# A graph, attention and expert layer on one core: TensorE's loop over chunk pairs in the first phase is written out

## The reference

```python
xn = _layernorm(x)
# graph part: two GCN layers with A = counts of edges plus self loops, D = degrees
h = relu(D^-1/2 A D^-1/2 (xn @ W1.T) + b1)
g = D^-1/2 A D^-1/2 (h @ W2.T) + b2
# attention with 256 random features per head, 12 heads of 64
q, k, v = split(xn @ W_qkv)
phi(t) = exp(t @ rf.T - 0.5 * |t|^2) / 16
out = phi(q) @ (phi(k).T @ v) / (phi(q) @ sum(phi(k)) + 1e-6)
m = layernorm(xn + out @ W_proj + b_proj) * gamma + beta
x = x + g + m
# expert part: top-2 routing of 8 experts, the higher index wins
x = x + silu(layernorm(x) @ w1[e]) @ w2[e]
```

## Time and profile before

| | |
|---|---|
| median of 3 runs | 2528.85 us |
| lowest, highest | 2526.37, 2531.22 us |
| the profiled execution's own time | 2527.59 us |
| its span in the trace | 2525.8 us |
| mean granted TensorE clock | 0.975 |
| TensorE busy | 2350.2 us (93%) |
| VectorE busy | 1261.0 us (50%) |
| ScalarE busy | 870.3 us (34%) |
| GpSimd busy | 866.3 us (34%) |

### The profile page before, as it was taken

One profiled execution on the slowest core, in us unless ns is written; L12 is line 12 of the kernel. 1 busy time (PEld: TensorE's weight loads), 2 busy tenths in 40 slices (PEclk: granted clock), 3 DMA queues, 4 the chain that ended last, 5 costly groups with the idle time before them and its releaser, 6 DMA issues.

```text
span 2525.8 us, 45448 instructions
## 1 busy us (share of the span) xinstructions
PE 2350.2 (93%) x16783; PEld 1590.9 (63%) x16783; DVE 1261.0 (50%) x2843; ACT 870.3 (34%) x1323; POOL 866.3 (34%) x615
## 2 busy tenths in 40 slices
PE   5999899998999999998999999999996899999576
PEld 3878687877666666664665666666663566666365
DVE  6757475734667676674114334443331344444344
ACT  3646364634637465471122222222210011111142
POOL 1001116567777787775601111111100000000265
PEclk9999999999999999998999999999998999999799
DMA  7779685654232323325307776677745844454187
GB/s 290 270 265 309 208 272 151 181 134 99 16 63 1 63 7 56 51 13 138 43 10 238 224 218 209 212 219 226 215 180 199 251 163 154 165 174 172 57 167 128
DMA packets 172999, 392.22 MB, mean 155 GB/s; under 512 B 74864, under 2 KB 81882, under 8 KB 166460
## 3 DMA queue, kind: packets, MB, share of 16 engines
q1 hardware_dynamic: 90796, 320.38, 36.8%
q0 software_dynamic: 71264, 40.45, 14.5%
q10 hardware_dynamic: 10800, 29.50, 3.0%
HBM read 226.03 MB, written 169.71 MB: 157 GB/s over the span
## 4 chain that ended last, share of the span: by engine, by line
PE 77%; DVE 8%; ACT 8%; issue 4%; DMA 3%; SPq 0%; POOL 0%; DVEq 0%; ACTq 0%; POOLq 0%
PE pair L1842 31%; PE pair L374 30%; PE pair L1674 4%; PE pair L1654 2%; PE pair L1604 2%; DVE arena L1306 2%; DVE arena L1308 2%; DVE arena L1312 2%; ACT arena L912 2%; DMA arena<-ahl_dram 1%; PE pair L1986 1%; PE pair L1663 1%; PE pair L1973 1%; ACT arena L896 1%; PE pair L1773 1%
## 5 line engine op out<-in xcount | busy, mean ns | idle before, releaser
L374 PE MATMUL pair<-arena 128*128 128x384 f16 (+2 forms) x5760 | 906.2, 319 | 25.4 <-SPq L363 12.8
L718 POOL DMA_INDIRECT cells<-arena x392 | 654.6, 1670 | 574.3 <-DMA cells<-arena 437.6
L1842 PE MATMUL pair<-arena 128*128 128x384 f16 x4900 | 819.2, 328 | 34.5 <-DMA arena<-ahl_dram 19.8
L374 PEld LDWEIGHTS pair<-arena 128*128 128x128 f16 (+1 forms) x5760 | 567.1, 99 | 347.8 <-issue 24.4
L1842 PEld LDWEIGHTS pair<-arena 128*128 128x128 f16 x4900 | 475.3, 98 | 344.1 <-issue 21.2
L750 POOL DMA_INDIRECT slots<-arena x25 | 28.7, 1149 | 513.6 <-DVEq L1530 481.0
L1674 PE MATMUL pair<-arena 128*128 128x66 f32 x1200 | 157.9, 275 | 4.8 <-ACT arena L872 4.3
L1674 PEld LDWEIGHTS pair<-arena 128*128 128x128 f32 x1200 | 146.6, 192 | 13.8 <-ACT arena L872 12.0
L872 ACT ACTIVATE arena<-pair,arena 128x256 f32<-128x256 f32 x300 | 123.6, 472 | 64.6 <-PE pair L1654 62.1
L736 POOL DMA_DIRECT2D arena<-cells x25 | 30.3, 1213 | 336.4 <-DMA arena<-cells 329.7
L987 ACT ACTIVATE arena<-arena 128x768 f32<-128x768 f32 x25 | 23.4, 935 | 344.7 <-DVE arena L1409 344.7
(11 more groups left out here) (202 smaller groups left out, 2425.0 us busy)
## 6 DMA issues: line engine op xcount, KB each, us to landing
cells<-arena SPq DMA_DIRECT2D x50, 800.0 KB, 9.9
ahl_dram<-arena SPq DMA_DIRECT2D x25, 1600.0 KB, 10.9
arena<-ahl_dram SPq DMA_DIRECT2D x25, 1600.0 KB, 7.7
arena<-in_x SPq DMA_DIRECT2D x70, 384.0 KB, 3.7
arena<-key_dram SPq DMA_DIRECT2D x28, 896.0 KB, 5.8
arena<-cells SPq DMA_DIRECT2D x25, 800.0 KB, 7.6
arena<-cells POOLq DMA_DIRECT2D x25, 800.0 KB, 7.5
split_w<-arena SPq DMA_DIRECT2D x32, 384.0 KB
```

Of the source, the lines that this page charges most:

```text
L374: ins = nc.tensor.matmul(dst[half], left(k, a), right(k, b, half), start=start and n == 0, stop=stop and n == 2)
L718: nc.gpsimd.indirect_dma_start(cells[k], bass.IndirectOffsetOnAxis(ap=idx_all[:, m:m + 1], axis=0), val_all[:, m:m + 1], None, bounds_chec ...
L1842: ins = nc.tensor.matmul(pair[u][:, half, 0:HD], a[:, 0, s * P:(s + 1) * P], X[part][:, s, half * HD:(half + 1) * HD], start=(s == 0 and p ...
```

## The change

TensorE's first phase is written out for the five chunks, with the chunk's number as a constant. Nothing else in the source changes.

```diff
-            with pe.Fori(0, (C - 1) // 2) as i:
-                chunk1(2 * i, 0)
-                chunk1(2 * i + 1, 1)
-            chunk1(C - 1, 0, False)
+            for c in range(C):
+                chunk1(c, c % 2, c + 1 < C)
             finish_phase(pe, 0)
```

## The result

| | before | after |
|---|---|---|
| median | 2529.15 us (5 runs) | 2513.65 us (5 runs) |
| lowest, highest | 2526.37, 2531.22 | 2512.74, 2516.51 |
| profiled execution, own time | 2527.59 | 2516.24 |
| its span | 2525.8 | 2514.5 |
| ratio | | 0.9942, 95% interval 0.9928 to 0.9957 |

The change makes the kernel faster by 0.58%, that is 10.9 to 18.2 us by the interval.

The account below looks back on a forecast made before the run. TensorE was taken to bound the kernel; 7.00 + 1.83 + 0.8 = 9.63 us off the profiled 2527.59 gave 2517.96, and 1.26 for the median of the runs made 2519.2 us. The range was 2515 to 2524 us.

Parts of the forecast that it names:

- What bounds the kernel: Whole kernel: TensorE is the bound, 77% of the chain, so time it gains in phase 1 is gained at the end.
- The jump back: Phase 1, border of chunks 1 and 2: TensorE's idle time at the loop's one taken jump goes, 7.00 us.
- The slow start: Chunk 2's first block of 216 matmuls, at half clock behind the jump, takes 34.31 instead of 36.14 us: 1.83 us gained.
- The opening: Start of phase 1: the loop's opening branch no longer delays the first matmul after the last weight split, 0.8 us gained.
- Chunk 0's block stays at 36.63 us: Phase 1's first 216 matmuls: no gain, since TensorE comes there from a pause that the change doesn't touch.
- Register computations: Address computations between matmuls in phase 1's loop body: removing them gains nothing, since TensorE's array covers them.
- Dips: TensorE's half-clock moments in phase 1, 1.63 us each: two may go or come, 3.3 us either way.
- the pause that is not the jump's: Rival, near 267 us: something unseen holds TensorE, so pause and slow start stay, 2528.1 us; chance 0.06.
- late engine: Rival, chunk 2: late row or weight loads make TensorE wait, returning up to 8.83 us; chance 0.08 for half or more.
- Straight code: Rival, chunks 2 and 3: late code fetches stall TensorE 8.83 us each, 2528.0 or 2536.9 us; slower has chance 0.04.

Follow-up runs that it names:

- run with quieter DMA: Kernel before, loop kept, with nine clears of the count matrix due late in chunk 1 moved three pairs later; 2527.54 us, ratio 0.9993.
- short-pause run: Changed kernel with phase 2 written out, plus 47 semaphore increments on TensorE between chunks 1 and 2; 2524.95 us, ratio 0.9984 to the kernel before.
- two other variants without the pause: Changed kernel with chunks 0 and 1 in a one-pass loop, 2515.25 us; or with a tiny two-pass loop between chunks 1 and 2, 2514.01 us.

## Why the prediction was right and wrong

The direction and the mechanism were right. The step that failed is the sum: it took one trace's 7.00 and 1.83 us as the price of the pause and its slow start, and put the dips at nothing, as a spread of 3.3 us to either side that only widened the range. The runs showed 7.8 and 2.2 us, and 2.8 us less inside chunks 2 and 3, to the same side in every trace of the two kernels.

- *What bounds the kernel*: right. Phase 1 became shorter by 11.78 us between the two first traces, and phases 2 to 5 took 1900.56 us against 1900.14. Over all traces phases 2 to 5 vary from 1893.3 to 1903.0 us, so two traces alone would not have shown this within 1 us; the means are 1898.8 us (three of before) and 1898.1 (two of the changed kernel).
- *The jump back, 7.00 us*: the right mechanism, sized from one execution. Three traces give 7.00, 8.11 and 8.25, mean 7.79. The run with quieter DMA (4.50) and the packets of q8 show what it depends on. I took the price of one trace as the price, and gave no bounds to it.
- *The slow start, 1.83 us*: right for that trace. The block takes 36.63 and 36.74 us in the other two, so 2.32 and 2.43, mean 2.19; with pauses that I made it was 1.72 and 2.81.
- *The opening, 0.8 us*: right, 0.88 became 0.10.
- *Chunk 0's block stays at 36.63 us*: it is 36.63, 37.01 and 36.20 in the traces of before, and 35.89, 36.03, 36.02 and 35.64 in those of the changed phase 1. But in the short-pause run, which opens phase 1 as the changed kernel does, it is 36.94, so a gain there is not shown. Chunk 0 as a whole has means of 117.68 and 117.35 us.
- *Register computations, nothing*: right; 115.01 and 114.07 us with, 115.02 and 114.09 without.
- *Dips*: here the prediction failed most. Chunk 3 lost one in each of four traces (1.71 us as a mean), and chunk 2's came at a pair where it costs less (1.05 beyond the slow start, together with small waits for VectorE). That is 2.76 us. It belongs to these two kernels and not to the jump: two other variants without the pause have four dips in phase 1. So that the dips came out in favour of the change was luck, as far as these runs tell.
- Sum by the runs: 7.79 + 2.19 + 2.76 us, and 0.17 in chunks 0, 1 and 4, are 12.91 us behind the first matmul. That is the difference between the mean lengths of phase 1 (591.97 over three traces, 579.07 over four). With the opening it is 13.7 us. The medians differ by 15.5 us in the first comparison and 14.05 in the second; where the rest of up to 1.8 us lies, no run shows.
- *The rivals*: the pause that is not the jump's is out (it went with the jump). No late engine took anything back: TensorE waits 4.7 us for ScalarE (4.3 before) and 0.2 for VectorE's marks. (The prediction's 2528.1 us for it should be 2519.2 + 8.83 = 2528.0.) Straight code shows no new "issue" pause in any of its traces, with DMA as busy as at the jump. The changed kernel's window behind the border of chunks 1 and 2, columns as in the earlier trace rows:

```profile
270.00:280.00 10.00, 10.00 (x63) 6.05 (x62) 0.13 (x1) 1.69 (x2) 1.55 (x1) 1.00 1.04 397
```
- The sum was also set against a single profiled execution and then moved to the median of three runs. The executions of one kernel differed by 4.9 and 3.8 us in that comparison, and the two that were profiled first lay on opposite sides of their medians. The low end of the range, 2515, left room for the dips, but not for a pause and slow start longer than one trace's besides.

On the Trainium skill's rules: its price of a compare-and-branch ("Advanced Engine Details and Errata", "Control Flow Timing"), about 108 ns, was not measured alone by any run, but 0.82 us for an opening and a near jump, and no gap in phase 2, say that a jump to a near target is cheap; for phase 1's jump the traces show 7.0 to 8.2 us. Its rule on fetching ("Runtime: NRT & Kernel Launch", "Instruction fetch mechanics"), with its 2048 instructions for TensorE, has the trace on its side three times: no gap with 588 matmuls and their weight loads in the body, 1.38 us with 1176, 7.0 to 8.2 with 1620. The counts of q8 agree with it: the two larger bodies are fetched again, the smallest is not.

## What to carry to other kernels

Look at what the bounding engine does where a loop jumps back. With a large body (here 1176 and 1620 matmuls, not 588) its code is fetched again, and the pause was 1.4 to 8.2 us, the long ones with DMA busy; behind the long ones matmuls at half clock cost some 2 us more. Write out such a loop, or make its body small; keeping DMA quiet at that moment shortened the pause to 4.50 us but did not end it. A loop that shows no gap is left alone, and register addresses cost nothing here. Size a pause from more than one execution, above all one that hangs on DMA, and compare the whole timeline of two traces: more than 2 us of this gain lay away from the pause.

## What the runs showed of the hardware

- The same taken jump costs 7.00, 8.11 or 8.25 us with DMA near 1.00 of its time, 4.50 with DMA at 0.5 before it. In these four traces the first matmul comes 4.8 to 5.3 us after the first packet of its code starts to move.
- TensorE's queue q8 moves 92 packets of 16 KB with the loop of 1620 matmuls and 87 without it: the jump back makes the body be fetched a second time. For the loop of 588 it does not.
- The half-clock moments of TensorE in steady work: all of them, in phase 1 of all 13 traces, sit on the first features behind the degrees' small matmuls. One costs 1.6 to 1.7 us at the middle pairs, and some 0.9 at the last (an estimate: chunk 2 with one there takes 115.02 us, chunk 3 with none 114.08). Of the 30 distances between them 24 are 95 to 144 us; the others go from 58 to 239.
- 140 semaphore increments on TensorE's sequencer took 20.75 us, 47 took 7.10: 0.15 us each.
